# A transformer layer on one core: three weight pieces move behind the first stacks, and one packed weight unit loads ahead of a wait for stores

## What is computed

```python
qkv = einsum('bsh,oh->bso', x, w_qkv)            # 16 heads of 32
scores = where(causal, einsum('bhqd,bhkd->bhqk', q, k) * scale, min)
attn = einsum('bhqk,bhkd->bhqd', softmax(scores), v)
x = layernorm(x + einsum('bsh,oh->bso', attn, w_o))
gate, up = x @ Wg.T, x @ Wu.T                    # Wg, Wu: 4096 x 512, unpacked from 4-bit codes
out = (gelu(gate) * up) @ Wd.T                   # Wd: 512 x 4096, the same packing
x = layernorm(x + out)
```

## Time and profile before

| | |
|---|---|
| time, three runs | 2673.74 us median (2673.54 to 2674.86) |
| the profiled execution | 2674.77 us, span 2672.9 us |
| mean granted TensorE clock | 0.991 of full speed |
| busy share | PE 98%, PEld 81%, DVE 65%, ACT 43%, POOL 39% |
| instructions | 41044 |

### The profile page before, as it was taken

The page is one execution under the profiler, slowest core; times in us unless marked ns, Lnnn a source line. Parts: engine busy times, 40 slices in busy tenths (PEclk is TensorE's granted clock), DMA queues, the critical chain, the costliest instruction groups (busy, mean ns, idle before and its releaser), DMA issues.

```text
span 2672.9 us, 41044 instructions
## 1 busy us (share of the span) xinstructions
PE 2612.9 (98%) x14322; PEld 2177.0 (81%) x14322; DVE 1739.2 (65%) x3504; ACT 1154.1 (43%) x2616; POOL 1044.4 (39%) x1160
## 2 busy tenths in 40 slices
PE   7999999999789999999999999999999999999998
PEld 6777887778468888888888888788888888888887
DVE  5777777777779888886333333655555575555656
ACT  4666666666644444443233323323333342333332
POOL 1444434443634444333444444523223242323333
PEclk9999999999799999999999999999999999999999
DMA  8676876778466665566555554466555546555552
GB/s 249 183 186 172 218 212 171 191 194 227 112 228 229 216 223 209 203 235 244 214 205 187 218 201 174 175 231 247 170 181 203 191 170 228 211 180 181 192 203 75
DMA packets 180061, 530.43 MB, mean 198 GB/s; under 512 B 14480, under 2 KB 72976, under 8 KB 157072
## 3 DMA queue, kind: packets, MB, share of 16 engines
q1 hardware_dynamic: 179856, 527.82, 59.6%
HBM read 378.86 MB, written 148.90 MB: 197 GB/s over the span
## 4 chain that ended last, share of the span: by engine, by line
PE 70%; DVE 2%; DMA 1%; issue 1%; POOL 0%; ACT 0%; SPq 0%; POOLq 0%; DVEq 0%; ACTq 0%
PE bank L1140 23%; PE bank L1141 23%; PE bank L1142 23%; PE bank L452 0%; PE bank L438 0%; DVE acc L1647 0%; DMA x1T_scratch<-x_late 0%; DMA scale<-down_scales 0%; DVE bx_l L1598 0%; DVE bstats L1788 0%; POOL probs L743 0%; DMA wd<-w_scratch 0%; DVE hid L1750 0%; PE bank L419 0%; PE bank L462 0%
## 5 line engine op out<-in xcount | busy, mean ns | idle before, releaser
L743 POOL TENSOR_SCALAR probs<-probs,row_inv 128x128 f32<-128x128 f32 (+3 forms) x512 | 263.0, 533 | 366.2 <-DVE row_inv L664 366.2
L1955 POOL TENSOR_TENSOR inter_l<-hid,inter_h 128x512 fp32r<-128x512 f32 x144 | 192.9, 1340 | 540.9 <-ACT inter_h L1316 540.8
L1140 PE MATMUL bank<-bx_h,wg 128*128 128x512 f32 x896 | 350.9, 392 | 1.0 <-ACT u_g L1316 1.0
L1141 PE MATMUL bank<-bx_l,wg 128*128 128x512 f32 x896 | 350.3, 391 | 0.0
L1140 PE MATMUL bank<-bx_h,wu 128*128 128x512 f32 x896 | 349.4, 390 | 0.0
L1141 PE MATMUL bank<-bx_l,wu 128*128 128x512 f32 x896 | 349.2, 390 | 0.0
L1142 PE MATMUL bank<-bx_h,wu 128*128 128x512 f32 x896 | 348.6, 389 | 0.0
L1142 PE MATMUL bank<-bx_h,wg 128*128 128x512 f32 x896 | 348.6, 389 | 0.0
L1750 DVE TENSOR_TENSOR hid<-hid,bank 128x512 f32<-128x512 f32 x192 | 131.9, 687 | 299.4 <-PE bank L1142 298.3
L1657 DVE TENSOR_TENSOR acc<-acc,bank 128x512 f32<-128x512 f32 x392 | 263.4, 684 | 94.3 <-PE bank L1142 84.3
L1960 POOL TENSOR_TENSOR inter_l<-hid,inter_h 128x512 fp32r<-128x512 f32 x112 | 146.0, 1303 | 368.6 <-ACT inter_h L1316 368.6
(11 more groups left out here) (173 smaller groups left out, 6015.0 us busy)
## 6 DMA issues: line engine op xcount, KB each, us to landing
wg<-w_scratch SPq DMA_DIRECT2D x48, 1792.0 KB, 9.2
wu<-w_scratch SPq DMA_DIRECT2D x48, 1792.0 KB, 13.1
q_st<-qk_scratch SPq DMA_DIRECT2D x128, 256.0 KB, 5.0
k_st<-qk_scratch SPq DMA_DIRECT2D x128, 256.0 KB, 7.0
w_scratch<-wg SPq DMA_DIRECT2D x16, 1792.0 KB, 8.2
w_scratch<-wu SPq DMA_DIRECT2D x16, 1792.0 KB, 10.6
b_slot<-t_scratch SPq DMA_DIRECT2D x112, 256.0 KB, 3.4
b_slot<-w_scratch SPq DMA_DIRECT2D x84, 256.0 KB, 2.8
```

Source lines behind the costliest of these rows:

```text
L743: pool.tensor_scalar(p, p, row_inv[:, h % 4, k:k + 1], 1.0, ALU.mult, ALU.mult).then_inc(norm_done, 1)
L1140: pe.matmul(out, a(0), b(0), start=start, stop=False, skip_group_check=True)
L1141: pe.matmul(out, a(0), b(1), start=False, stop=False, skip_group_check=True)
L1955: pool.tensor_tensor(inter[1][:, m, t, :], hid[:, 2 * m + t, :], f32(inter[0][:, m, t, :]), ALU.subtract).then_inc(inter_split, 1)
```

## The change

In the prologue SP loads five pieces ahead of the projections. Piece 5 is issued behind the reads of stack 0, pieces 6 and 7 behind those of stack 1. ACT and DVE take piece 5 at the head of slot 2 of batch 0, piece 6 at the head of slot 5, piece 7 at the head of slot 6. In the hand-over unit 8 is loaded in `start(31)`, ahead of SP's wait for the stores; in step 1 ACT's `spread(7)` and `take_u2(1, "g")` move ahead of `sums_high(2, 0)`, and DVE's `unpack(7)` moves ahead of `gate_up_low(2, 0)`, so ahead of `add_down(0, 1)` too.

```diff
+    LATE_PIECES = {2: 5, 5: 6, 6: 7}
...
-            for i in range(1, len(PIECES)):
+            for i in range(1, 5):
                 load_w(i)
...
                     read_stack(1, c)
+
+                    for i in ((5,), (6, 7))[c]:
+                        load_w(i)
...
-                if use + 3 < len(PIECES):
+                if use < 2:
                     w_part(use + 3)
...
                 for s in range(SLOTS):
+                    if b == 0 and s in LATE_PIECES:
+                        w_part(LATE_PIECES[s])
...
+            if n == 31:
+                load_unit(8)
...
-                        if k + 5 < UNITS * NG:
+                        if 8 < k + 5 < UNITS * NG:
                             load_unit(k + 5)
...
+                if j == 1:
+
+                    spread(7)
+                    take_u2(j, "g")
                 if prep:
                     sums_high(j + 1, 0)
-                take_u2(j, "g")
+                if j > 1:
+                    take_u2(j, "g")
                 split_high(j - 1, 1, 1)
                 gelu(j, 0, 0)
                 take_u2(j, "u")
                 split_high(j - 1, 0, 1)
-                if j == 1:
-
-                    spread(7)
...
                 if j < NG:
                     down_low(j)
+                if j == 1:
+                    unpack(k + 1)
                 if prep:
                     gate_up_low(j + 1, 0)
                 times_up(j, 0, 0)
                 if ended:
                     refine(st - 1, 1)
                 add_down(j - 1, 1)
-                if j == 1:
-                    unpack(k + 1)
```

## The result

The changed kernel takes 2680.39 us in the median of 8 runs (2678.49 to 2684.51). The kernel before, on the same chip, takes 2674.9 us (8 runs, 2673.16 to 2676.21). The ratio is 1.0023, 95% interval 1.0012 to 1.0034: slower by 5.5 us by the medians, 6.1 us by the ratio. The forecast was 2675.7 us. The execution that was profiled took 2681.63 us, its span 2679.8 us; against the profiled execution of before that is 6.9 us more.

The account below looks back on a forecast made before the run. PE was busy 98% of the span, so only its waits and low clock could matter. Part A's +5.15 us and part B's -3.2 us gave +1.95 us on the 2673.74 us median: 2675.7 us, range 2668.5 to 2680.5.

Parts of the forecast that it names:

- The rival of a late unit 7: Hand-over: unit 7 landing after 787 delays unpack(7) and add_down(0, 1); sum +5.8 us, 2679.5 us; chance 0.15.
- Part A: First 50 us and the parts in slots 5 and 6: 1.65 + 1.5 + 2.0 = +5.15 us, bounds +1.7 to +8.2.
- The first write lands at 19.0, stack 0 goes out 2.85 us earlier, slot 0 at 30.5: Start: with three pieces less ahead, q's first write lands sooner; PE's wait before slot 0 shrinks to about 2 us.
- The low clock at slot 0 may go: Slot 0: the 1.5 us lost to the low clock behind PE's wait may go; low clock counted once, behind slot 3.
- q2's write lands at 50.0, PE goes on 1.65 us later: Slot 3: pieces 6 and 7 ahead add 3.0 us to the write; PE goes on at 51.7 after idling near 7.8 us.
- The rival that the writes are not held up: Start: q2's write passes pieces 6 and 7, keeping the gain at slot 0; -5.6 us, 2668.1 us; chance 0.15.
- The parts in slots 5 and 6, 2.0 us: w_part(6) and w_part(7) heading slots 5 and 6 on ACT and DVE: between 0 and 4.9 us, taken as 2.0.
- Part B: The hand-over: -4.9 + 1.7 = -3.2 us.
- Unit 8 lands at 789.5 and no longer sets `add_down(0, 2)`; `take_u2` gives 0.9 us: Hand-over: unit 8 lands six us earlier; 0.9 of the 0.97 us wait for take_u2 goes.
- `unpack(7)` sticks out by 1.5 us, `add_down(0, 1)` ends at 790.4, `down(0, 3)` waits 2.4 us: Hand-over: unpack(7) on DVE mostly fills an idle hole; its excess makes a new PE wait of 2.4 us.
- With no long idle time the low clock behind 798 goes: Hand-over: the low clock behind PE's old wait for add_down(0, 2) disappears, 1.5 us gained.
- `seed(2, "g")` waits for unit 10, +1.7 us: Hand-over, p6 of step 2: PE comes 4.9 us earlier but unit 10 does not keep up; 1.7 us taken back.

Follow-up runs that it names:

- run 5: Run 4 with piece 5 issued behind the second write of q instead of behind stack 0; 2672.69 us against 2674.43 for the kernel before, ratio 0.9993.
- run 9: The start of run 5 joined to the hand-over of run 6; 2670.07 us against 2673.76 for the kernel before, ratio 0.9985.
- run 10: Run 9 with POOL held back until add_down(0, 1) is done; 2673.34 us against 2673.76 for the kernel before, ratio 0.9998.
- run 4: Run 3 with pieces 6 and 7 issued in slot 2 behind q3's write, not behind stack 1; 2674.29 us against 2674.6 for the kernel before.
- run 3: Run 1 with w_part(6) and w_part(7) both heading slot 7, loads not moved; 2680.02 us against 2674.6 for the kernel before, ratio 1.0019.
- run 11: Kernel before, all pieces loaded at the start, only w_part(6) and w_part(7) moved to slots 5 and 6; 2677.16 us against 2673.76, ratio 1.001.
- run 1: The changed kernel's start alone, hand-over as before; 2682.74 us against 2674.6 for the kernel before, ratio 1.003.
- run 8: Run 2 with POOL waiting for add_down(0, 1) before its work of step 1; 2672.05 us against 2674.43 for the kernel before, ratio 0.999.
- run 2: The changed kernel's hand-over alone, prologue as before; 2672.77 us against 2674.6 for the kernel before, ratio 0.9994.
- run 6: Run 2 with DVE's unpack(7) left behind add_down(0, 1), as before; 2669.77 us against 2674.43 for the kernel before, ratio 0.9984.
- run 7: The kernel before with only the load of unit 8 moved earlier; 2671.7 us against 2674.43, ratio 0.9989.

## Why the prediction was wrong

The direction of each half was right and both sizes were off in the slow direction: in the trace the start cost 8.0 instead of 5.15 us, and the hand-over gave 0.5 instead of 3.2 us. Three terms of the sum were mis-sized: the delay of q2's write by the two pieces, the parts in slots 5 and 6, and, the largest, the new wait for `add_down(0, 1)`, which was 4.98 instead of 2.4 us because the subtractions ahead of it do not keep their duration beside POOL. The measured 2680.39 us is 0.1 us inside the range and 4.7 us above the forecast; 1.2 us of that is the kernel before, whose median was 2673.74 us in three runs and 2674.9 us in eight. The rival of a late unit 7 has a time near the measured one (2679.5), but that is chance: its cause did not occur.

**Part A, by its steps.**

- *The first write lands at 19.0, stack 0 goes out 2.85 us earlier, slot 0 at 30.5.* Half right. The reads went out earlier still, q's by 4.0 and k's by 3.25 us, yet slot 0 began at 32.00. I had moved the start of PE by as much as the reads. From the issue of k's reads to slot 0 it took 11.6 us instead of 9.7. This repeats: 9.6 to 10.0 us in the six executions that load all pieces at the start, 11.0 to 11.6 in the four with piece 5 right behind stack 0, and 10.5 to 10.9 in the three with piece 5 later (runs 5, 9, 10). So piece 5 explains the smaller part, and why reads that go out earlier take longer to land stays open. Of the 1.3 us that are left a part is the execution: slot 0 of those six began between 31.96 and 33.34 us.
- *The low clock at slot 0 may go.* Not so: 6 matmuls in 2 us, as before. That it was counted once, behind slot 3, came true for 1.6 us of the table (+3.31 to +4.89), so the 1.5 us stand.
- *`w_part(5)` in slot 2 is nothing.* Right in the sum: it shows as 1.54 us of PE's idle time, inside the time that slot 3 would have taken anyway. In 4 and 5 the stall is gone and this wait is still there (1.54 us in both); what it costs there was not tried.
- *q2's write lands at 50.0, PE goes on 1.65 us later.* **This is the first term of part A that was mis-sized.** The write was issued when forecast (40.52 for about 41) and landed at 51.68; PE went on 3.3 us later, at 53.32. Two things make the other 1.65 us. The reads of stack 1 went out 0.8 us earlier (34.88 against 35.68), not 1.35. And from these reads to the landing of the write it took 16.8 us instead of 12.7: the two pieces ahead of it cost 4.1 us, where their bytes at 348 GB/s gave 3.0. (Between the traces of runs 3 and 4 the same difference is 3.6 us.) The long issue of this write, 1.14 us, is not the cause: in run 3 it took 0.42 us, and the write landed at 51.59. Runs 3 and 4 show that the mechanism is this one: with the two pieces, and SP's issue of them, taken away from ahead of the write the stall is gone. The rival that the writes are not held up fell with it. The stall itself was 4.81, not 7.8 us, because PE came to it later than forecast: 1.3 us of lead instead of 4.4 (the reads and the low clock), and 1.5 of it spent in slot 2.
- *The parts in slots 5 and 6, 2.0 us.* **Right in kind, too small.** Run 11 gives +3.4 us and run 3 against 1 gives 2.7; in the trace it is 0.7 in slot 5, 2.1 in slot 6, and 0.4 more in a low clock that I had not counted. I had taken the middle of the bounds 0 and 4.9 with slot 5 hidden.

By the rate into 128 partitions that the Trainium skill (DMA: Bandwidth & Descriptors, Bandwidth) gives, 341 GB/s, taken for the stacks as well, part A was an estimated -2 us. The changed kernel is 8 us slower there, so the rates of the trace were the ones to go by.

**Part B, by its steps.**

- *Unit 7 has landed by about 784.* Right: `spread(7)` ends its wait at 790.94, 783.6 in before's time (less the 7.35 us by which the changed kernel is late). The rival of a late unit 7 fell.
- *Unit 8 lands at 789.5 and no longer sets `add_down(0, 2)`; `take_u2` gives 0.9 us.* Right. `spread(8)` ends its wait at 797.08, 789.7 in before's time. PE's wait for `take_u2` is gone from its timeline, and the offset falls by 1.1 us at 786.3.
- *`unpack(7)` sticks out by 1.5 us, `add_down(0, 1)` ends at 790.4, `down(0, 3)` waits 2.4 us.* **This is the step that failed in its mechanism.** `add_down(0, 1)` ended at 800.12, 792.8 in before's time, and the wait was 4.98 us. The excess of unpacking was right, and run 8 measures the wait that it leaves alone: 2.29 us. The other 2.7 us are `gate_up_low(2, 0)`: I took its subtractions at the duration they had before. There POOL's split of the lows began at 786.62, when the first two of them were over and the third, begun at 786.52, was under way. Moved 1.5 us later (less what PE's wait for `take_u2` gives), all three fall beside POOL's work. Run 2 shows the same wait with the prologue of before, so the start has no part in it.
- *With no long idle time the low clock behind 798 goes.* It followed from the step above and fell with it: PE comes back from 4.98 us at 0.50.
- *`seed(2, "g")` waits for unit 10, +1.7 us.* Not borne out. No wait stands at that place in the changed kernel, nor in run 6, where PE is earlier: unit 10 landed there by 807.42, 4.1 us before its time of 811.52. Its landing moved with the rest. This error went the other way, and hid 1.7 us of the miss by chance.

The -0.45 us of the trace are made up so: -1.24 from `take_u2`, +5.08 for the new wait with the matmul behind it, -4.71 for the old one, and +0.42 for the low clock, which costs 1.94 us behind the new wait and cost 1.52 behind the old. How sure is this number? Runs 1, 3, 4, 5 and 11 leave the hand-over as it was. Counted in the same way, from 782 us to the end, their traces come out at +2.3, +0.4, +1.7, -0.5 and +1.7 us against before's: in some of them the low clock behind the old wait lasted longer. So one trace does not tell the worth of the hand-over to better than 2 us. By the medians it gives 1.8 us alone (run 2), and 2.0 to 2.6 us on top of the changed start (8.1 us in run 1 against 5.5 to 6.1). The lengths of the new wait, 4.98 and 4.95 us, do not vary so, and they are the miss.

Run 7 shows that unit 8 alone is worth 1.4 us of PE's waits there; run 6, which leaves `unpack(7)` behind `add_down(0, 1)`, is worth most. Of its 4.7 us by the medians its trace has 2.6 us at the hand-over, and 1.3 us ahead of it, where the code is that of before.

**What stays open.** Run 6 joins an earlier `take_u2` to an early unit 8; `take_u2` alone was not run. Runs 5 and 6 should have given -6.4 us together and gave -3.7; the intervals are each about 2.5 us to both sides, and at the hand-over the traces of 9 and 6 give the same (2.7 and 2.6 us), so no loss between the two halves is shown. The low-clock stretches at the end of attention moved one trace (run 7) by 4.0 us, for reasons that the rows do not show. Differences below 2 us therefore rest on the medians, or on the length of a wait in a trace, and not on ends of spans.

## What to carry to other kernels

A load that is moved to a later place in a queue is not free because the engine does not need it yet: look at which store stands behind it in the queue, and at who waits for that store. A DVE instruction that is moved brings its old duration only if POOL is as idle at the new place as at the old one; read POOL's row at the time to which it goes. And work put at the head of a slot can cost most of its length where both its engines are on the way to the mask or copy that TensorE waits for (2.1 of 2.3 us in slot 6, but 0.7 in slot 5), and once more where the clock falls behind the idle time.

## What the runs showed that was not expected

- Subtractions of DVE with two SBUF tiles ran at 0.68, 0.42 and 1.22 us with POOL idle (run 8) and at 1.79, 1.48 and 1.74 us beside POOL's elementwise work: 1.11, 1.06 and 0.52 us more, so the addition does not grow with the size of the tile. In the kernel before, the third of them had begun 0.1 us ahead of POOL's split and kept its 1.22 us; in run 6 the second had begun 0.04 us behind it and took 1.53. The two adds behind them (`hid`, `acc`), which read a PSUM bank, kept 0.67 us while POOL was still busy. The Trainium skill (SBUF — State Buffer, SBUF: two separate sides) says that DVE and GpSimd share one pair of ports, that the instruction which starts first holds it to its end, and that a DVE instruction with two SBUF inputs needs it against a GpSimd one that reads SBUF. The rows agree with it, in which instructions suffer and in what they suffer.
- A write of 512 KB took 3.6 us in the quiet and 11.2 us behind a stack and two pieces.
- A stall of 1.84 us in slot 6 was followed by the 0.50 clock, in the changed kernel and in run 11; the 1.75 us in slot 3 of the kernel before were followed by 1.00 in each stretch from 50 to 56 us. The length of a wait alone did not tell whether the clock would fall; a stretch's own row has to be read.
